# A linear-attention block with a feed-forward network: queries of six token blocks placed behind the context sums, eight places for x's high parts, first rows loaded before a weight unit

## The reference

```python
Q, K, V = x @ wq.T, x @ wk.T, x @ wv.T            # D = 64
energy  = einsum('bnd,bne->bde', K, V)            # 64 x 64, a sum over all 4096 tokens
context = (Q @ energy) * sqrt(3 / D)
x = layernorm(x + context @ wo.T)
h = silu((x @ w1.T) * s1) * ((x @ w2.T) * s2)     # 256 -> 1024
h = gelu((h @ h1.T) * t1)                         # 1024 -> 1024
h = gelu((h @ h2.T) * t2)
x = layernorm(x + (h @ w3.T) * s3)                # 1024 -> 256
```

## Time and profile before

| what | us |
|---|---|
| time, median of 3 runs | 658.42 (658.38 to 658.77) |
| time of the profiled execution | 660.88 |
| its span, first to last instruction | 659.0 |
| PE busy | 639.4 |
| DVE, ACT, POOL busy | 477.1, 411.3, 279.3 |

### The profile page before, as it was taken

How to read it: one execution, slowest core, us unless ns; L and a number is a source line. 1 busy time by engine, 2 the same in 40 slices (tenths; PEclk the granted TensorE clock), 3 DMA queues, 4 the chain that set the end, 5 groups by cost and what they waited for, 6 DMA issues and landing times.

```text
span 659.0 us, 9226 instructions
## 1 busy us (share of the span) xinstructions
PE 639.4 (97%) x3187; PEld 536.0 (81%) x3187; DVE 477.1 (72%) x713; ACT 411.3 (62%) x696; POOL 279.3 (42%) x226
## 2 busy tenths in 40 slices
PE   9989888999999999999999999999999999999995
PEld 7868676887879888888889888888888888888885
DVE  4576565798755898598755899598746799488476
ACT  5479786857863557656763457655764456666654
POOL 0367799188000466069000367059000268069024
PEclk9999998999999999999999999999999999999999
DMA  8989899953330025734330015734340005534201
GB/s 318 379 337 354 308 377 355 345 193 128 128 130 1 1 70 160 258 128 176 133 132 1 1 35 170 274 128 142 132 174 1 0 8 185 191 128 146 111 1 66
DMA packets 24370, 103.89 MB, mean 158 GB/s; under 512 B 2224, under 2 KB 3312, under 8 KB 16496
## 3 DMA queue, kind: packets, MB, share of 16 engines
q1 hardware_dynamic: 24032, 102.98, 44.1%
q10 hardware_dynamic: 288, 0.26, 0.1%
HBM read 87.51 MB, written 23.07 MB: 168 GB/s over the span
## 4 chain that ended last, share of the span: by engine, by line
PE 72%; DVE 3%; POOL 1%; issue 1%; ACT 1%; POOLq 0%; DVEq 0%; ACTq 0%
PE ps L1285 48%; PE ps L1233 13%; PE ps L1331 8%; DVE R L925 1%; DVE xr L909 1%; PE ps L1165 1%; PE ps L1153 1%; PE ps L1354 0%; ACT R L663 0%; DVE U L944 0%; POOL rstd L476 0%; POOL quarter L504 0%; ACT quarter L709 0%; POOL rstd L447 0%; POOL quarter L513 0%
## 5 line engine op out<-in xcount | busy, mean ns | idle before, releaser
L1285 PE MATMUL ps<-R,ring 128*128 128x512 f32 x1792 | 411.2, 391 | 5.3 <-issue 4.2
L1285 PEld LDWEIGHTS ps<-R,ring 128*128 128x128 f32 x1792 | 336.5, 188 | 75.7 <-issue 4.6
L925 DVE TENSOR_TENSOR R<-quarter,R 128x512 fp32r<-128x512 f32 x284 | 250.4, 903 | 69.7 <-ACT R L663 69.5
L663 ACT CAST R<-quarter 128x512 fp32r<-128x512 f32 x288 | 175.3, 615 | 31.0 <-POOL quarter L504 12.0
L1233 PE MATMUL ps<-x1T,w 128*128 128x512 f32 x512 | 119.6, 392 | 1.2 <-issue 0.6
L709 ACT ACTIVATE quarter<-U,sc 128x512 f32<-128x512 f32 x96 | 69.5, 723 | 72.9 <-DVE U L944 32.1
L1233 PEld LDWEIGHTS ps<-x1T,w 128*128 128x128 f32 x512 | 95.2, 188 | 23.4 <-ACT sg L629 1.7
L494 POOL TENSOR_TENSOR quarter<-quarter,quarter 128x512 f32<-128x512 f32 x32 | 49.2, 1538 | 103.0 <-ACT quarter L709 96.4
L629 ACT ACTIVATE sg<-ps,sc 128x512 f32<-128x512 f32 x64 | 43.9, 689 | 62.8 <-PE ps L1233 62.7
L445 POOL TENSOR_TENSOR ve<-mv,eps 128x4 f32<-128x4 f32 x14 | 5.7, 405 | 181.9 <-DVE mv L902 181.9
L679 ACT COPY U<-ps 128x512 f32<-128x512 f32 x96 | 56.3, 586 | 36.8 <-PE ps L1285 35.0
(11 more groups left out here) (84 smaller groups left out, 373.1 us busy)
## 6 DMA issues: line engine op xcount, KB each, us to landing
ring<-combos SPq DMA_DIRECT2D x56, 1024.0 KB, 4.9
combos<-unit SPq DMA_DIRECT2D x8, 1024.0 KB, 9.0
unit<-in_h1T SPq DMA_DIRECT2D x4, 1024.0 KB, 14.0
xr<-in_x_rows SPq DMA_DIRECT2D x8, 512.0 KB, 5.0
unit<-in_h2T SPq DMA_DIRECT2D x4, 1024.0 KB, 8.4
xT<-in_xT SPq DMA_DIRECT2D x7, 512.0 KB, 8.0
out<-xr SPq DMA_DIRECT2D x7, 512.0 KB, 2.9
w<-w_dram SPq DMA_DIRECT2D x3, 1024.0 KB, 7.6
```

The costliest lines, as they stand in the source:

```text
L663: nc.scalar.copy(R[slot_of(p, u)][:, 0, c, :], quarter[operand_home(p, u)][:, c, :]).then_inc(hi_done, 1)
L925: nc.vector.tensor_tensor(r[:, 1, c, :], quarter[operand_home(p, u)][:, c, :], r[:, 0, c, :].bitcast(f32), ALU.subtract).then_inc(lo_done, 1)
L1285: last = nc.tensor.matmul(ps[:, bank + j, :], w, view(R[slot_of(p, u)][:, part, k, :]), start=n in (0, 1, 5) and k == 0 and part == 0, sto ...
```

## The change

`Q_BETWEEN` goes from 4 to 2: the queries of blocks 2 and 3, which were between the sums of the `front`, are put behind them, with those of blocks 4 to 7. The pieces are dealt out anew around T1, block 0's attention and its transposes. The high parts of x get eight buffers instead of four; the four new ones lie over the ring's first two slots, so the first ring load now waits for the last query. SP loads the rows of block 0 before unit 0 instead of behind the loads of w1 and w2. ACT's bit sums are moved between other work, that of unit 1 from ahead of block 0's transposed tiles to behind the first `silu`. DVE's subtraction for block 7 no longer waits for T1. `flag_sum(1)` on PE goes to the end of the stage, and `flag_out(1)` on DVE behind `lo_of_transposed(0, 6)`.

```diff
-Q_BETWEEN = 4
+Q_BETWEEN = 2
-        xhi = [over(f"xhi{i}", x1T_at + 4096 * i, [P, EC, BLK], f32r) for i in range(4)]
+        xhi_at = [x1T_at + 4096 * i for i in range(4)] + [ring_at + 4096 * i for i in range(4)]
+        xhi = [over(f"xhi{f}", xhi_at[f], [P, EC, BLK], f32r) for f in range(NB)]
@@ load_ring
+                if g == 0:
+                    sp.wait_ge(q_ready, NB)
@@ SP's list
+            load_rows(0)
             load_unit(0)
             load_w12(0)
             load_w12(1)
-            load_rows(0)
             load_unit(1)
@@ high_x, on ACT
-                if f >= 4:
-                    act.wait_ge(q_ready, f - 3)
@@ ACT's list
-            for f in range(4):
+            for f in range(5):
                 high_x(f)
             hi_of_q(0)
-            high_x(4)
+            high_x(5)
             hi_of_q(1)
-            high_x(5)
-            raw_q(2)
             high_x(6)
-            raw_q(3)
             high_x(7)
             bits_of_whole(0)
-            bits_of_w12(0)
-            bits_of_w12(1)
             act.wait_ge(t1_ready, 1)
             nc.scalar.activation(T1s[:, 0, :], ...).then_inc(t1_hi, 1)
+            raw_q(2)
+            bits_of_w12(0)
+            raw_q(3)
+            bits_of_w12(1)
             raw_q(4)
-            bits_of_w12(2)
-            bits_of_w12(3)
-            raw_q(5)
             for q in range(ACT_TILES[0]):
                 normalise_tile(0, 0, q, q + 1, tile_norm[0])
-            bits_of_whole(1)
+            raw_q(5)
+            bits_of_w12(2)
             raw_q(6)
+            bits_of_w12(3)
             hi_of_transposed(0, 6)
             raw_q(7)
             for j in range(HC):
                 silu(0, j, A)
                 if j == 0:
+                    bits_of_whole(1)
+                if j == 1:
                     bits_of_whole(2)
@@ DVE's list
-            dve.wait_ge(t1_ready, 1)
             low_x(NB - 1)
+            dve.wait_ge(t1_ready, 1)
             dve.wait_ge(t1_hi, 1)
@@
             normalised_tilewise(0, 0, attention_residual)
+            lo_of_transposed(0, 6)
             flag_out(1)
-            lo_of_transposed(0, 6)
             residual1(1, 4)
@@ PE's list, end of front
-                q_pieces(range(16, 18), view)
+                q_pieces(range(8, 10), view)
                 ... T1 ...
-                q_pieces(range(18, 23), view)
+                q_pieces(range(10, 16), view)
                 ... block 0's attention ...
-                q_pieces(range(23, 28), view)
+                q_pieces(range(16, 27), view)
                 transposed_first(0)
-                q_pieces(range(28, 30), view)
+                q_pieces(range(27, 29), view)
                 transposed_first(1)
-                q_pieces(range(30, 32), view)
-                pe.wait_ge(tile_sum[0], 1)
-                flag_sum(1)
+                q_pieces(range(29, 31), view)
                 transposed_first(2)
                 attention_half(0)
                 transposed_first(3).then_inc(tr_ready, 1)
+                q_pieces(range(31, 32), view)
                 attention_half(1).then_inc(op_ready, 1)
+                pe.wait_ge(tile_sum[0], 1)
+                flag_sum(1)
```

More of the change, by code:

```diff
@@ L105, in build @@
         w3 = sb("w3", [P, HC, E], f32r)
+        ring_at = top[0]
         ring = sb("ring", [P, SLOTS, KH, HALF], f32r)
@@ L566, in high_x @@
                     act.wait_ge(x_first, 16)
-                if f >= 4:
-                    act.wait_ge(q_ready, f - 3)
-                nc.scalar.copy(xhi[f % 4].rearrange("p c (t n) -> p c t n", t=TPB), tiles_of(xT[f])).then_inc(xhi_done, 1)
+                nc.scalar.copy(xhi[f].rearrange("p c (t n) -> p c t n", t=TPB), tiles_of(xT[f])).then_inc(xhi_done, 1)
             def bits_of_w12(i):
@@ L859, in low_x @@
                 dve.wait_ge(xhi_done, f + 1)
-                nc.vector.tensor_tensor(tiles_of(xlo[f]), tiles_of(xT[f]), xhi[f % 4].bitcast(f32).rearrange("p c (t n) -> p c t n", t=TPB),
+                nc.vector.tensor_tensor(tiles_of(xlo[f]), tiles_of(xT[f]), xhi[f].bitcast(f32).rearrange("p c (t n) -> p c t n", t=TPB),
                                         ALU.subtract).then_inc(xlo_done, 1)
@@ L1025, in _ @@
             nc.vector.tensor_copy(ET[:, :, :], ps[0:D, 2, 0:D].unsqueeze(1).broadcast_to([D, 2, D])).then_inc(et_out, 1)
+            low_x(NB - 1)
             dve.wait_ge(t1_ready, 1)
-            low_x(NB - 1)
             dve.wait_ge(t1_hi, 1)
@@ L1114, in q_pieces @@
                         pe.wait_ge(xlo_done, b + 1)
-                    x = xhi[b % 4][:, c, :] if part == 0 else tiles_of(xlo[b])[:, c, :, :]
+                    x = xhi[b][:, c, :] if part == 0 else tiles_of(xlo[b])[:, c, :, :]
                     last = nc.tensor.matmul(ps[:, Q_BANK[b], :], wqr[:, c, :] if view is exact else wq[:, c, :], view(x),
```

## The result

The changed kernel takes 667.23 us (median of 4 runs, 666.5 to 667.91), the kernel before 658.4 us beside it. The ratio is 1.0137, with a 95% interval of 1.0119 to 1.0154: 8.8 us slower. The profiled execution took 666.5 us, with a span of 664.6 us.

A forecast was written before the change was run, and what follows sets the result against it. The prediction took the front as bound by when POOL finishes `combine(1)`, which holds SP's transfers. The larger delay, +8.0 us, made the profiled 660.88 us 668.9; less 2.46 over the median, 666.4, 8-in-10 range 662.8 to 669.0.

The forecast's parts named there:

- Queries moved: Front on PE: eight pieces leave the part ahead of T1, so block 0's attention starts about 1.7 us earlier.
- Rows before unit 0: Front loads: unit 0 and `combine(0)` come 1.37 us later; POOL reaches the deviations at 35.0 to 35.8, no shift taken.
- ACT's order: ACT behind the normalised tiles: two query copies and two bit sums put the cast at 41.29, 0.78 us late.
- The flag: Ahead of layer 1: flag done at 43.5, load and branch cost 0.95 us, so layer 1 starts at 44.45, before 41.41.
- rival C: PE's clock falls to 1.2 GHz ahead of layer 1, first tile 0.94 us longer: 667.3 us; chance 0.10.
- Unit 1's bit sum and `combine(1)`: Behind the first `silu`: `combine(1)` begins at 47.45, 7.95 us late, and so do the transfers behind unit 1's store.
- PE's own delay: Block 1's transposes slip to 55.8, PE 4.8 us late; it waits about 7 us for the ring load.
- Nothing gives this back: Behind 101 us no engine recovers the +8.0 us; POOL, ACT and DVE are late by less than PE.
- A: Layer 1 starts on time, the flag's late place costing nothing; 5.4 us of delay left: 663.8 us; chance 0.10.
- B: The wait at 97 us is not the ring's; PE's own 4.8 us decide: 663.2 us; chance 0.06.
- D: Transfers behind unit 1's store catch up all delay before 101 us, so the kernel gets faster: 656.7 us; chance 0.05.
- E: No change, catching up and losses cancel: 658.4 us; chance 0.03.

The follow-up runs named there:

- before, first trace: The kernel before, unedited, in its first traced execution: 660.88 us.
- before, second trace: The kernel before, unedited, traced once more: 657.78 us.
- before, bit sum late: The kernel before with only unit 1's bit sum on ACT moved behind the first `silu` of layer 1: 665.95 us against 658.48.
- before, flag late: The kernel before with only PE's `flag_sum(1)` behind `attention_half(1)` and DVE's `flag_out(1)` behind `lo_of_transposed(0, 6)`: 658.34 us against 658.48.
- changed, bit sum back: The changed kernel with unit 1's bit sum directly behind the two normalised tiles again: 660.73 us against 658.48.
- changed, DVE's flag back: The changed kernel with `flag_out(1)` before `lo_of_transposed(0, 6)` again, PE's flag sum staying at the end: 666.02 us against 658.05.
- changed, rows back: The changed kernel with block 0's rows loaded behind w1 and w2 again: 666.82 us against 658.05.
- mended: The changed kernel with unit 1's bit sum and DVE's flag early again, two w1/w2 bit sums between other work: 656.49 us against 657.86.
- changed, copies first: The changed kernel with SP issuing the two copies of h1's halves (2 MB) before it waits for `combine(1)`: 660.31 us against 658.48.
- before, copies first: The kernel before with SP issuing the two copies of h1's halves before it waits for `combine(1)`: 656.19 us against 657.86.
- mended, copies first: The mended kernel with SP issuing the two copies of h1's halves before the wait for `combine(1)`: 657.39 us against 657.86.

## Why the prediction was right

The forecast was 666.4 us in a range of 662.8 to 669.0; the measured median is 667.23. Its main step is shown and not only argued. In every trace with the old order of transfers, the ring load of the fourth hidden product lands 60 to 62 us behind the start of `combine(1)`, whatever PE did in between:

| kernel | `combine(1)` begins | load lands | difference | fourth product |
|---|---|---|---|---|
| before, first trace | 39.50 | 101.15 | 61.7 | 101.29 |
| before, second trace | 39.58 | 100.13 | 60.6 | 100.21 |
| before, bit sum late | 44.54 | 104.93 | 60.4 | 105.03 |
| before, flag late | 40.04 | 100.72 | 60.7 | about 100.7 |
| changed | 46.81 | 107.59 | 60.8 | 107.66 |
| changed, bit sum back | 38.20 | 99.54 | 61.3 | about 103.2 |
| changed, DVE's flag back | 44.32 | 105.17 | 60.9 | 105.24 |
| changed, rows back | 45.24 | 106.33 | 61.1 | 106.47 |
| mended | 38.05 | 98.16 | 60.1 | 98.25 |
| changed, copies first | 47.14 | 102.54 | 55.4 | 102.67 |
| before, copies first | 39.60 | 96.75 | 57.2 | about 98.5 |
| mended, copies first | 38.56 | 96.60 | 58.0 | about 97.9 |

Only the last three rows break it, and there 2 MB of transfers were taken out of the chain. In eight of the traces PE waits for this product, and in all eight it goes on 0.07 to 0.14 us behind the landing; in the other four it comes later than the landing or with it and does not wait. What is constant is the landing and not the way there: with the old order the load took between 10.7 us (bit sum back, where PE freed its slot late) and 16.3 us from issue to landing. It stands behind the bytes issued before it.

Step by step:

- *Queries moved.* Right: block 0's attention begins 2.1 us earlier (30.93), I had 1.7.
- *Rows before unit 0.* The term was +1.37 us, too large. `combine(0)` begins at 25.8 to 27.5 us in the five traces of kernels built on the one before, and at 27.3 to 28.1 in the six built on the changed one with the rows in front, a difference of the means of about 1.0. But the first trace, from which I counted, had it late already (27.34), so it came to 27.49 and not 28.7, with one slow step (2.16) instead of two. The step that failed is its consequence: "the earlier attention gains nothing". POOL began the deviations at 33.70 instead of 35.34, and the front gained 1.6 us. That `combine(0)` is what POOL's deviations wait for in the changed kernel is right (POOL has no idle time between the two), and with the rows back they come 0.57 us earlier.
- *ACT's order.* Right: from the tiles to the cast 3.04 us (36.59 to 39.63), I had 3.06.
- *The flag.* Right: 1.04 us from the flag to layer 1, I took 0.95. It started 1.65 us earlier than forecast for the reason above.
- *The clock.* This was rival C, with a chance of 0.10, and it came beside the forecast: layer 1's start ran at 1.2 GHz, and the first `silu` came 2.14 us behind layer 1's start where I had 1.15. It gave back 1.0 of the 1.65 us.
- *Unit 1's bit sum and `combine(1)`.* +7.3 us, I had +7.95. From the store (+7.2) to the ring load's issue (+6.6) and landing (+6.4) the queue made up 0.8 us.
- *PE's own delay.* I had 4.8 us and a wait of 7 us. PE came to the fourth product at 102.76, 5.7 us late, and waited 4.90: block 1's transposes were 4.1 us late, and the clock fell once more ahead of the hidden products (1.6 us). It changed nothing, since the larger of the two delays counts.
- *"Nothing gives this back."* Nearly right: of the 6.4 us at the fourth product 0.2 came back by a shorter slow stretch behind it and 0.6 at 190 us, where the first trace has a wait of 0.59 us and the changed kernel none.
- *The sum.* It came out well by two errors that cancel. Profile to profile the change cost 5.6 us (666.5 against 660.88), not 8.0. But I carried the first trace's 2.46 us over the median along as a constant. It came from the wait and the low clock of that one execution, and the delay of the transfers takes the place of both. (The last 0.7 us of the 8.8 is that the changed kernel's profiled execution lies below its own median.) Against the second trace the spans differ by 8.6 us: 7.45 us at the fourth product, 1.4 us for the clock behind it, and about 0.3 us made up later. That the forecast met the median within 1 us is therefore in part luck.

Of the rivals, A fell with the flag experiment (its place does delay layer 1, by 2.6 us) and B with the table above. D and E needed the queue to catch up, and it made up 0.8 of 7.2 us.

## What to carry to other kernels

Before moving a small operation, find what waits for it on the other engines and what those have queued in order behind that wait: here a bit sum of 1.2 us held POOL, POOL held a store, and the store held a saturated chain of transfers on which PE waits in the end. Of the time in which a transfer queue stands idle just before a long saturated stretch little comes back (here 0.8 of 7.2 us), so transfers that wait for nothing belong ahead of those that wait. And where a wait is sometimes followed by a fall of the clock and sometimes not, take a second trace before using one execution's excess over the median as a constant.

## What the runs showed of the hardware

The fall of PE's clock is not a function of the idle time alone. The same wait of 2.10 to 2.12 us for the bit sum ahead of layer 1's last 12 products was followed by a fall in six traces (those 12 products took 4.30 to 4.61 us) and by none in the other six (3.0 us), and for the kernel before it was once the one and once the other. Of five waits of 2.6 to 2.7 us ahead of layer 1, four were followed by a fall; all waits of 3.6 us and more were. Of three waits of 2.02 to 2.04 us ahead of block 1's transposes one was (rows back: granted clock 0.50 from 55 to 57 us), and waits of 1.5 us and less ahead of block 1 and of the fourth product were not. One fall cost PE between 1.3 and 2.6 us: 1.3 to 1.6 us over layer 1's last 12 products, 1.4 to 2.5 us over its first 40 (10.73 to 11.84 us against 9.34), 1.4 to 2.6 us over the 96 products behind the ring's wait (23.42 to 24.61 us against 22.01). The Trainium skill, TensorE: Matmul & The Clock Gate ("HAM oscillation — how this bites in real kernels"), says that waits between bursts of matmuls throttle the clock so that the next burst starts slowly; these traces agree, and show it for waits as short as 2.0 us.
